# The last batch's half scans: one scan for two rows, state carried by ScalarE, loads on another queue, another side order

## What is computed

```python
xz = einsum('bld,ed->bel', x, in_proj_w); xs, z = halves of xz      # 1024 inner channels each
xs = silu(causal_conv_4_taps(xs) + conv_b)
dt_lo, B, C = split(xs @ x_proj_w.T)                                  # 32, 16 and 16 columns
delta = softplus(dt_lo @ dt_proj_w.T + dt_proj_b)
h[t] = exp(delta[t] * A) * h[t-1] + delta[t] * B[t] * xs[t]           # 16 states per channel
y[t] = sum over states of h[t] * C[t]
y = (y + xs * D) * silu(z)
x1 = layernorm(x + y @ out_proj_w.T)
top 2 of 8 experts by x1 @ gate_w.T, softmax over the two
out = layernorm(x1 + weighted sum of (x1 @ expert_w[e].T + expert_b[e]))
```

## Time and profile before

| | us |
|---|---|
| timed runs, median of 3 | 2286.59 |
| lowest, highest | 2284.71, 2302.08 |
| profiled execution: its span, first to last instruction | 2281.1 |
| lowest timed run less that span | 3.6 |
| median less that span | 5.5 |

### The profile page before, as it was taken

How to read it: one execution, slowest core, us unless ns; L and a number is a source line. 1 busy time by engine, 2 the same in 40 slices (tenths; PEclk the granted TensorE clock), 3 DMA queues, 4 the chain that set the end, 5 groups by cost and what they waited for, 6 DMA issues and landing times.

```text
span 2281.1 us, 30428 instructions
## 1 busy us (share of the span) xinstructions
PE 2037.1 (89%) x8624; PEld 1201.8 (53%) x8624; DVE 1983.3 (87%) x2191; ACT 1660.2 (73%) x3074; POOL 1850.8 (81%) x1505
## 2 busy tenths in 40 slices
PE   8896779789898989999899989999799998879998
PEld 3444455455554645545555555645455555545543
DVE  5899999899999989898899899899898988889911
ACT  5758858677598856988588876989579785666534
POOL 2959999589898979889898889899898897686503
PEclk9896879889999999999999999999999999769999
DMA  5513143158854776557754687556855575466875
GB/s 169 180 47 92 38 139 111 51 172 252 278 129 143 241 255 180 143 168 257 256 152 119 201 266 234 129 180 216 284 149 141 180 252 209 123 209 215 278 278 120
DMA packets 222085, 412.79 MB, mean 181 GB/s; under 512 B 29880, under 2 KB 36152, under 8 KB 221920
## 3 DMA queue, kind: packets, MB, share of 16 engines
q1 hardware_dynamic: 180448, 322.36, 42.1%
q0 software_dynamic: 20496, 57.16, 12.3%
q10 hardware_dynamic: 20976, 31.33, 4.1%
HBM read 299.37 MB, written 85.72 MB: 169 GB/s over the span
## 4 chain that ended last, share of the span: by engine, by line
POOL 25%; PE 10%; issue 9%; DMA 7%; DVE 7%; ACT 3%; SPq 1%; ACTq 0%; DVEq 0%; POOLq 0%
POOL hst L1704 12%; PE bank L1137 8%; POOL first_dbu L1704 4%; DMA y<-scaled 2%; DVE hst L1755 2%; DVE y L1744 2%; POOL delta L1675 2%; POOL u L1678 2%; DVE hst L1920 1%; DMA Bbc<-b_scratch 1%; POOL ysb L1630 1%; DVE u L1775 1%; PE hTp L1153 1%; POOL zs L1649 1%; ACT dA L1563 1%
## 5 line engine op out<-in xcount | busy, mean ns | idle before, releaser
L1563 ACT ACTIVATE dA<-delta,negA 128x512 f32<-128x512 f32 (+1 forms) x1146 | 712.2, 636 | 307.9 <-DVE hst L1755 248.2
L1704 POOL TENSOR_TENSOR hst<-u,Bbc 128x512 f32<-128x512 f32 x666 | 870.7, 1412 | 42.3 <-PE hTp L1153 26.9
L1755 DVE TENSOR_TENSOR_SCAN hst<-dA,hst 128x512 f32<-128x512 f32 x672 | 791.0, 1211 | 50.9 <-ACT dA L1563 46.9
L1153 PEld LDWEIGHTS hTp<-ident,hst 128*128 128x128 f32 x4096 | 498.3, 149 | 325.6 <-issue 140.4
L1153 PE MATMUL hTp<-ident,hst 128*128 128x128 f32 x4096 | 560.1, 288 | 106.0 <-DVE hst L1755 33.7
L1744 DVE SCALAR_TENSOR_TENSOR y<-hTp,Ct,y 128x1024 f32<-128x1024 f32 x463 | 587.1, 1268 | 69.4 <-PE hTp L1153 54.9
L1704 POOL TENSOR_TENSOR first_dbu<-u,Bbc 128x512 f32<-128x512 f32 x222 | 292.9, 1393 | 42.0 <-DVE hits L1836 29.2
L1755 DVE TENSOR_TENSOR_SCAN hst<-dA,first_dbu 128x512 f32<-128x512 f32 x224 | 263.3, 1210 | 9.5 <-ACT dA L1563 7.0
L1137 PE MATMUL bank<-wslot,hidT 128*128 128x512 f32 x512 | 244.3, 610 | 10.4 <-ACT zs L1459 5.0
L1137 PE MATMUL bank<-wslot,tokT 128*128 128x512 f32 x480 | 234.6, 617 | 9.7 <-ACT tokT L1474 9.7
L1137 PE MATMUL bank<-delta,tokT 128*128 128x512 f32 x480 | 220.8, 593 | 0.0
(11 more groups left out here) (187 smaller groups left out, 2874.8 us busy)
## 6 DMA issues: line engine op xcount, KB each, us to landing
wslot<-in_w_expT SPq DMA_DIRECT2D x90, 1024.0 KB, 6.5
Bbc<-b_scratch SPq DMA_DIRECT2D x113, 256.0 KB, 3.5
wslot<-in_w_inT SPq DMA_DIRECT2D x26, 1024.0 KB, 6.1
y<-scaled POOLq DMA_DIRECT2D x49, 512.0 KB, 5.3
zs<-sorted_tokens ACTq DMA_DIRECT2D x91, 256.0 KB, 5.1
sorted_results<-ysb SPq DMA_DIRECT2D x90, 256.0 KB, 6.2
res<-in_w_expT SPq DMA_DIRECT2D x18, 1024.0 KB, 6.9
gate_scratch<-zs SPq DMA_DIRECT2D x64, 256.0 KB, 2.1
```

Source lines behind the costliest of these rows:

```text
L1153: mm = nc.tensor.transpose(hTp[q % 2][:, tok(j)], hst[n % 2][:, j, start:start + P], ident[:, :])
L1563: nc.scalar.activation(decay_of(step, halved), delta[w.odd][:, j, cols], ACT.Exp, scale=negA[:, j, n:n + 1]).then_inc(exp_done, 1)
L1704: nc.gpsimd.tensor_tensor(dbu_row(n, j), u[w.odd][:, j, :], Bbc[n % 2][:, :], ALU.mult).then_inc(dbu_done, 1)
L1755: nc.vector.tensor_tensor_scan(hst[n % 2][:, j, :], dA[j % 2][:, :], dbu_row(n, j), 0.0, ALU.mult, ALU.add).then_inc(scan_done, 1)
```

## The change

1. In the last batch, one scan of 512 columns takes two rows of 256 (two channel groups of one state, one half of the tokens). In column 0 of the upper row the decay is zero, so the recurrence starts anew there. The exponential of an upper row writes columns 1 to 255 only; column 0 of the upper row is zeroed once in each `dA` tile.
2. In the second half the lower row still starts from a tile. For the upper row ScalarE adds decay x carried state to the product's first column (`head`), one 128x1 operation per pair, after a wait for GpSimd's product of that pair. The decays of that column come from four exponentials of 128x16 (`turn_decay`). 16 copies of 128x8 keep the first half's last columns (`carried`).
3. `hst` holds a state's half as a flat strip; `columns` goes.
4. `szE` and the two Wo blocks (`WoE`) are issued from ScalarE's queue; `load_Wo` leaves the list, and `load_res` is a group of its own.
5. The planner: VectorE's row counts double, costs follow the new scans and heads, more than two turned pieces may stand between two state transposes (with a wait for the eviction of the one two places before, `in_row`), and ScalarE takes turned pieces in TensorE's order.
6. `SEG_EPI` has new bonuses and a pace of 0.252 in place of 0.15.

The diff, cut to its core:

```diff
-        "gy": [] if alone else [("pool", 1.4, [..., (("szE", k // HALF), "sp", 8), ...])],
+        "gy": [] if alone else [("pool", 1.4, [..., (("szE", k // HALF), "act", 6), ...])],
-        "szE": [("sp", 0.5, [])],
+        "szE": [("act", 0.35, [])],
+        "WoE": [("act", 0.7, [])],
...
-    every = {"sp": 8, "pool": 2} if halved else {"sp": 8}
+    every = {"sp": 8, "pool": 2, "dve": 2} if halved else {"sp": 8}
...
-                return ended(("scan", r // 2 * 2 - 3), "dve") if r > 3 else True
+                return (r < 4 or ended(("scan", r // 2 * 2 - 3), "dve")) and (r < STEPS or r % 2 == 0 or ended(("dbu", r // 2), "pool", 0.1))
...
-            cost = 0.45
+            cost = 0.65 if r > STEPS and r % 2 else 0.45
...
-            return len([y for r, y, _ in rows["pe"] if r == row and y[0] in TURNED]) < 2 and added.get(row, 1e9) + 0.1 <= now
+            here = [y for r, y, _ in rows["pe"] if r == row and y[0] in TURNED]
+            return added.get(row, 1e9) + 0.1 <= now and (len(here) < 2 or ended(here[-2], "act", 0.1))
...
-                tokens += pace if e == "dve" else 0
+                tokens += pace * every.get(e, 1) if e == "dve" else 0
...
+                if halved and e == "act" and x in turns and not all(ended(y, "act") for y in turns[:turns.index(x)]):
+                    continue
...
-          ... "lz": each("szE", NT), ...
+          ... "lz": [("szE", 0), ("szE", 1), ("WoE",), ("szE", 2), ("szE", 3)], "lr": named(MIX, "load_res"), ...
-SEG_EPI = Segment(by_urgency({"lz": 66977, "L0": -107229, "ld": 67022, "oe": -16774, "of": -17404, "ln": 50444, "sc": 47088, "wt": 31041, "we": 72523, "w2": 27267, "ww": 8736, "nz": -20788, "bi": -50819, "L1": -158950, "EE": 5557, "EF": 148016, "h0": 63625, "h1": 20853, "h2": -58415, "h3": 13355, "hl": -11051, "hd": -8221, "m5": -193015, "m6": 13327, "hm": -96262}), 0.15,
+SEG_EPI = Segment(by_urgency({"lz": 203, "L0": 129, "lr": 78, "oe": 130, "of": -136, "ln": 88, "sc": 196, "wt": 214, "we": -113, "w2": -131, "ww": 282, "nz": 58, "bi": 115, "L1": 77, "EE": 129, "EF": -31, "h0": 77, "h1": 0, "h2": -36, "h3": -23, "hl": -11, "hd": 2, "m5": -16, "m6": -36, "hm": 263}), 0.252,
...
+        turn_decay = Ct[NB % 2]
...
+        def half_states(n):
+            return hst[n % 2].rearrange("p j t -> p (j t)")[:, 0:ND * HL]
+        def carried(n):
+            return hst[n % 2].rearrange("p j t -> p (j t)")[:, ND * HL + n // 2 * ND:ND * HL + (n // 2 + 1) * ND]
...
-                if not w.seg.steps and w.seg.turned[x] > 1:
+                if not w.seg.steps and w.seg.turned[x] > 1 or w.seg.steps and w.in_row(x) > 1:
                     pe.wait_ge(turned_taken, count - 2)
...
+                elif name == "szE":
+                    t = x[1]
+                    if t == 0:
+                        act.wait_ge(delta_ready, w.b * ND + ND)
+                        for k in range(2):
+                            act.wait_ge(z_stored[k], w.b * (16 * NT))
+                    elif t == PAIR:
+                        act.wait_ge(dbu_done, w.b * (NS * ND))
+                    act.dma_start(early_z(t, 0, HALF), z_dram[w.e, tok(t), :].rearrange("p (k n) -> p k n", k=HALF)).then_inc(early_in[t], 16)
+                elif name == "WoE":
+                    act.wait_ge(exp_done, w.b * (NS * ND))
+                    for h in range(HALF):
+                        s = w.weights(("Wo", h))[0]
+                        act.dma_start(slot_of(w, s), block_src(("Wo", h))).then_inc(w_loaded[s], 16)
...
+            def half_decay(w, step, n, j):
+                c, upper = step // STEPS, step % 2
+                cols = slice(c * HL + upper, (c + 1) * HL)
+                dst = decay_of(step, True)[:, upper:HL]
+                if step in (1, 3):
+                    nc.scalar.activation(decay_of(step, True)[:, 0:1], ones[:, 0:1], ACT.Copy, scale=0.0)
+                if step // ND == 2 and upper:
+                    nc.scalar.activation(turn_decay[:, j // 2, :], negA[:, j, :], ACT.Exp, scale=delta[w.odd][:, j, HL:HL + 1])
+                if not (c and upper):
+                    nc.scalar.activation(dst, delta[w.odd][:, j, cols], ACT.Exp, scale=negA[:, j, n:n + 1]).then_inc(exp_done, 1)
+                    return
+                nc.scalar.activation(dst, delta[w.odd][:, j, cols], ACT.Exp, scale=negA[:, j, n:n + 1])
+                head = half_dbu[step // 2 % 4][:, HL:HL + 1]
+                act.wait_ge(dbu_done, w.b * (NS * ND) + (step // 2 + 1))
+                nc.scalar.activation(head, carried(n)[:, j:j + 1], ACT.Identity, bias=head, scale=turn_decay[:, j // 2, n:n + 1]).then_inc(exp_done, 1)
...
+                    if w.seg.halved and step % ND == ND // 2 and 0 < step // ND <= NS:
+                        done = step // ND - 1
+                        nc.scalar.activation(carried(done), half_states(done)[:, HL - 1:ND * HL:HL], ACT.Copy)
...
-                    elif w.seg.halved:
+                    elif w.seg.halved and step % 2 == 0:
...
-                        nc.vector.tensor_tensor_scan(hst[n % 2][:, j, start:stop], decay_of(step, True), half_dbu[step // 2 % 4][:, step % 2 * HL:(step % 2 + 1) * HL],
-                                                     hst[n % 2][:, j, kept:kept + 1] if c else 0.0, ALU.mult, ALU.add).then_inc(scan_done, 1)
+                        nc.vector.tensor_tensor_scan(half_states(n)[:, j * HL:(j + 2) * HL], dA[step // 2 % 2][:, :], half_dbu[step // 2 % 4],
+                                                     carried(n % NS)[:, j:j + 1] if c else 0.0, ALU.mult, ALU.add).then_inc(scan_done, 2)
```

More of the change, by code:

```diff
@@ L284, in start_main @@
         what, cost = {"act": (("exp", r), 0.7), "pool": (("dbu", r), 1.3), "sp": (("B", r), 0.5), "pe": (("part", r), 1.05),
-                      "dve": (("scan", r), (0.6 if halved else 1.1) + (1.22 if r in part_number else 0))}[e]
+                      "dve": (("scan", r * every.get(e, 1)), 1.1 + (1.22 if r * every.get(e, 1) in part_number else 0))}[e]
         if halved and e == "act":
-            cost = 0.45
-        if e == "dve" and r in part_number:
-            added[r] = now + 1.22
+            cost = 0.65 if r > STEPS and r % 2 else 0.45
+        if e == "dve" and what[1] in part_number:
+            added[what[1]] = now + 1.22
+        if e == "dve" and halved:
+            done[("scan", what[1] + 1), e] = now + cost
         done[what, e] = free[e] = now + cost
@@ L417 @@
           "m0": TOKENS[:6], "m1": TOKENS[6:12], "m2": TOKENS[12:18], "m3": TOKENS[18:], "ZB": ZB, "Z": Z,
-          "m4": tokens(*range(LATE, TILES)), "lz": each("szE", NT), "oe": [x for x in MIX if x[0] in ("gy", "yT", "out") and x[1] < (2 if x[0] == "out" else 4)], "of": [x for x in MIX if x[0] in ("gy", "yT", "out") and x[1] >= (2 if x[0] == "out" else 4)],
+          "m4": tokens(*range(LATE, TILES)), "lz": [("szE", 0), ("szE", 1), ("WoE",), ("szE", 2), ("szE", 3)], "lr": named(MIX, "load_res"), "oe": [x for x in MIX if x[0] in ("gy", "yT", "out") and x[1] < (2 if x[0] == "out" else 4)], "of": [x for x in MIX if x[0] in ("gy", "yT", "out") and x[1] >= (2 if x[0] == "out" else 4)],
           "lb": named(PRO, "load_hx", "load_wx"), "nz": each("next_z", NT) + each("next_res", NT),
```

52 lines of the change are left out of this document (20 added, 32 removed).

## The result

| | before | after |
|---|---|---|
| median of the timed runs | 2285.65 us (4 runs, 2280.74 to 2302.08) | 2431.52 us (4 runs, 2430.35 to 2434.36) |
| profiled execution, span | 2281.1 us | 2428.6 us |

The ratio is 1.0625, 95% interval 1.0588 to 1.0662. The forecast was 2268 us, so the prediction was wrong: in size, in sign, and outside its range. The kernel lost 146 us.

The account below looks back on a forecast made before the run. Bound: VectorE and TensorE together in the last batch's segment, TensorE alone in the final stretch. Scans -10.2, idle -14, ScalarE +2, head's wait +1, issues +2, B rows +1 make -18.2 us: 2268 us, 8-in-10 range 2250 to 2292.

Parts of the forecast that it names:

- What bounds the kernel now: Opening step: all edits in the last batch's segment; VectorE idle 30.0 of 287 us there, TensorE alone bounds the final stretch.
- The new order: Last batch: route chain 14 us earlier and filler expert tiles take 14 us off VectorE's idle; bounds loss 12, gain 24.
- the 1.9: Last batch: new small VectorE idle, in us, said to include waits from a third transposed piece between two sums.
- the slow one: Rival, last batch's second half: ScalarE's heads stand on the path once over 0.37 us each; +16 us, 2303; chance 0.1.
- The scans: Last batch: merged scans at 1.12 and 1.18 us a pair save 3.2 and 7.0 us, together 10.2; bounds 0 and 20.5.
- 16 + 6: VectorE in the last batch's segment: 16 us idle left and 6 us new, beside 247 us work, making 269 of 287.
- The frame: Last batch: final stretch starts earlier only if VectorE and TensorE both finish earlier; a VectorE saving alone is mostly lost.
- TensorE isn't fed: Rival, last batch: route no earlier, its 60 us stay, scans' saving mostly waits at the end; -4 us, 2282; chance 0.21.
- Heads: Last batch's second half: 64 ScalarE operations at 0.30 us, 19 us, mostly fitting; with other small operations charged 2 us.
- Loads: Last batch: z rows and Wo on ScalarE's queue start the first gate product some 14 us earlier; issues charged 2 us.
- B rows: Last batch: a B row on ScalarE's queue behind 4 MB of loads; charged 1 us, at most 8.
- Final stretch: Kernel's end: again 113 us, bound by TensorE; over 116 us would mean work was only moved behind the scans.

Follow-up runs that it names:

- e1: Kernel after, with more than two turned pieces between state transposes allowed only in the last batch: 2296.11 us, ratio 1.0027.
- e2: Kernel before, with the planner's rule for more than two turned pieces added in all but the last batch's segment: 2422.85 us, ratio 1.058.
- e3: Kernel before, with only merged scans, carried states and heads on ScalarE; order and loads as before: 2286.56 us, ratio 0.9999.
- g3: e3 with only the four early z rows moved to ScalarE's queue: 2285.48 us, ratio 1.0012.
- e5: e1 with the B rows of states 2 and 3 of the last batch's first half on SyncE's queue: 2294.49 us, ratio 1.0021.
- c2: Kernel before, with planner bonus m1 changed from -1377 to -4377, another order without a pile or third turned piece: 2288.26 us, ratio 1.0009.
- c1: Kernel before, with planner bonus ln changed from 9049 to 6049, another order without third turned pieces: 2342.41 us, ratio 1.0235.

## Why the prediction was wrong, point by point

**The failed step** is in "What bounds the kernel now": "All edits lie in the last batch's segment", and with it "The new order", which put the third transposed piece "inside the 1.9". I had read the rule as part of the last batch. It is a line of a shared planner, without the `halved` of its neighbours. It makes some 135 of the 146 us by e1 and e2, and 143 of the 147.5 by the split of the two traces, in five batches that the sum did not contain. Of the rivals, none had it; the slow one was about ScalarE's heads.

**The scans: half right.** Pitch start to start, in the kernel after, first half and second half:

```profile
2044.22 2.33 DVE L1959 TENSOR_TENSOR_SCAN hst<-dA,scaled 128x512 f32<-128x512 f32 x2
2046.46 1.26 DVE L1785 SCALAR_TENSOR_TENSOR y<-hTp,Ct,y 128x1024 f32<-128x1024 f32 x1
...
2209.40 2.45 DVE L1959 TENSOR_TENSOR_SCAN hst<-dA,hst,first_dbu 128x512 f32<-128x512 f32 x2
2211.76 1.26 DVE L1785 SCALAR_TENSOR_TENSOR y<-hTp,Ct,y 128x1024 f32<-128x1024 f32 x1
```

That is 2.24 / 2 = 1.12 and 2.36 / 2 = 1.18, the two figures of the forecast. VectorE's 10.2 us were saved, nearly: over 287 us from the last batch's first scan its work is 247.2 us instead of 257.0, the forecast's "247". But its idle time went from 30.0 to 39.8 us, where the forecast had 16 + 6 (before, then after, columns as in the earlier trace rows):

```profile
1881.00:2168.00 287.00, 248.67 (x1098) 158.51 (x1097) 257.00 (x396) 180.65 (x425) 196.13 (x158) 0.87 0.64 208
```

```profile
2024.30:2311.30 287.00, 242.96 (x1076) 155.48 (x1075) 247.21 (x263) 201.70 (x508) 194.26 (x156) 0.88 0.65 208
```

e3 shows that the scans alone bought nothing (0.9999). The frame had said so: "a saving on VectorE alone ... is mostly lost". Then the sum counted all of it. The term should have been near 0, as in the rival *TensorE isn't fed*.

**Heads: right in size, and they hide in the kernel after.** In the second half of the kernel after, the heads of one product tile, and then two heads with what follows them on ScalarE:

```profile
L1601 ACT ACTIVATE scaled<-hst,scaled,Ct 128x1 f32<-128x1 f32 x32 | 12.0, 375 | 0.2
```

```profile
2200.30 0.37 ACT L1601 ACTIVATE first_dbu<-hst,first_dbu,Ct 128x1 f32<-128x1 f32 x1
2200.66 0.48 ACT L1596 ACTIVATE dA<-delta,negA 128x256 f32<-128x256 f32 x1
...
2201.47 0.37 ACT L1601 ACTIVATE first_dbu<-hst,first_dbu,Ct 128x1 f32<-128x1 f32 x1
2201.75 0.57 ACT L1479 ACTIVATE tokT<-hTp 128x512 f32<-128x512 f32 x1
```

A head lasts 0.375 us, but start to start it costs 0.28 to 0.36: the trap of the scans again. So the 0.30 of the forecast was about right, and under the 0.37 from which heads were to stand on the path. ScalarE is busy 101.9 of 138.3 us in that half and doesn't bound it, no scan there names an exponential or a head as its releaser, and e3's 2286.56 us is the opposite of 2303. It isn't so in every version: in g3 two second-half scans wait 6.7 us for a head, 4.9 and 1.8.

**Loads: first step right, then nothing.** After, the first gate product starts 8.0 us after the first scan (2032.32 and 2024.3); before, 20.9 us. That is the 13 us that were forecast as 14. But the gate matmuls came 98.2 us after the first scan, against 89.4 before, and the first expert matmul of the routed batch 150.2 us after, against 149.3. The lead of the first step was gone before the third. The 14 us of idle that I took off VectorE were never there: e3, which has none of it, and e1, which has all, differ by 10 us in the wrong direction.

**B rows: the sign was found and the size missed.** I charged 1 us, with the queue's wait as a bound of 8. The wait was 6.88 us on VectorE in e1, and 5.1 us in the kernel after. By e5, though, it was worth next to nothing in time.

**Final stretch: a little longer.** From the start of the last scan to the end it is 123.7 us (2304.9 to 2428.6) against 120.2 before. In e3, with the old order, it is 122.4 us, so part of what the scans save comes back there. With those 3.5 us the forecast's 113 becomes 116.5, just over the 116 that I had set as the sign of work only moved behind the scans.

**The low clock in the routing hole: still there.** After, 2110 to 2170 has 0.65 and 0.67, where 1970 to 2030 had 0.53 before. From the gate matmuls to the first expert matmul it is 52.0 us instead of 59.9, but the gate came 9 us later. So TensorE still isn't fed there. That speaks for the unfed rival as the account of the last batch, though its "60 us ... stay" isn't exact.

With the rule kept out, the forecast would have been 2268 against 2296 measured for e1: too low by 28, and over the upper end of its whole range, 2292 (by e1's ratio on the forecast's own baseline it is 2293). So the sum would have failed in the last batch as well; the steps are the 10.2 us of the scans, which bought nothing, and the 14 us of idle that stayed. By the number the unfed rival's 2282 and the head's 2303 are about equally near. The traces favour the unfed one; that it alone explains the last batch is argued, not shown.

## What to carry to other kernels

When a change touches a shared planner, list which of its outputs change before costing anything: compare the written-out order of every segment, and count the segments that repeat. A rule that looks like more freedom for one place can be what closes a row in another. With in-order engines, read an order by its longest pile between two steps of the main chain and by what each piece at the head of a queue waits for; a fitted order can be left in a harmless way (c2) and in a very costly one (c1). And a saving on one engine counts only in a stretch that this engine bounds.

## What the runs showed of the hardware

- TensorE's granted clock stayed under full speed long after a stretch of stalls. In a batch of e2 it fell from 1.00 to 0.71 in a stretch where TensorE was busy 13.35 of 20 us, idle once for 6.24 us behind a scan, and it stood at 0.81 and 0.83 over the 91 us after it, though TensorE was busy 78.7 of those.
- A 128 KB load behind 4 MB on one queue, with the DMA engines full, had two prices: the issue itself took 2.31 us (3.07 us in the kernel after), where that of nearly all other B rows took 0.33, and the data came 18.8 us after it instead of 4.1. On the other queue (e5) its issue took 0.37 us and its data 13.6 us.
- One scan of 512 columns costs 0.05 us less, start to start, than two of 256, and 0.11 less where the start is read from a tile.
